# Experts' rows added in memory, one block at a time, to one zeroed row per token

## The reference, cut to what matters

```python
aff = sigmoid(einsum('bsd,de->bse', x, wa))
topk_p, topk_i = top_k(aff, 2)                  # two of 16 experts for each token
topk_p = topk_p / sum(topk_p, axis=-1, keepdims=True)
combine = sum(one_hot(topk_i, 16) * topk_p[..., None], axis=2)
routed = einsum('bsed,bse->bsd', experts_all(x, rg, rgb, rw1, rb1, rw2, rb2), combine)
shared = sum(experts_all(x, sg, sgb, sw1, sb1, sw2, sb2), axis=2)
return x + shared + routed
```

## Time and profile before

| What | Value |
|---|---|
| Median of 3 runs | 1137.9 us (1137.3 to 1138.25) |
| Profiled execution, its own time | 1144.85 us |
| Its span, first to last instruction | 1143.1 us |
| Mean granted clock of PE | 0.944 |
| PE busy | 1029.8 us (90%) |
| DVE, ACT, POOL busy | 845.9 us, 684.2 us, 582.2 us |

### The profile page before, as it was taken

The page is one execution under the profiler, slowest core; times in us unless marked ns, Lnnn a source line. Parts: engine busy times, 40 slices in busy tenths (PEclk is TensorE's granted clock), DMA queues, the critical chain, the costliest instruction groups (busy, mean ns, idle before and its releaser), DMA issues. The chain is left out here.

```text
span 1143.1 us, 24593 instructions
## 1 busy us (share of the span) xinstructions
PE 1029.8 (90%) x9092; PEld 771.7 (68%) x9175; DVE 845.9 (74%) x1480; ACT 684.2 (60%) x1203; POOL 582.2 (51%) x635
## 2 busy tenths in 40 slices
PE   4899998689998998878999988789996999999997
PEld 4677776634443776557877766687673888888874
DVE  5589999869998788757888866698746455556548
ACT  4565773779886656567888764574543345545431
POOL 5444445425544344458778885303873355555520
PEclk9999999789999999979999998659999899999999
DMA  8584431869886223232222210764986577678879
GB/s 318 176 256 122 160 116 38 158 174 237 221 226 177 87 72 104 68 89 56 65 71 63 57 30 1 257 226 181 203 249 224 165 239 242 236 246 281 303 264 352
DMA packets 133705, 194.60 MB, mean 170 GB/s; under 512 B 67990, under 2 KB 70204, under 8 KB 132792
## 3 DMA queue, kind: packets, MB, share of 16 engines
q1 hardware_dynamic: 117256, 149.45, 43.3%
q0 software_dynamic: 8544, 24.68, 7.0%
q10 hardware_dynamic: 7792, 18.96, 5.3%
HBM read 127.47 MB, written 44.48 MB: 150 GB/s over the span
## 5 line engine op out<-in xcount | busy, mean ns | idle before, releaser
L470 PE MATMUL ps_y<-kv,toep 128*128 128x288 f32 x640 | 156.5, 407 | 5.2 <-DMA toep<-taps_padded 3.2
L470 PEld LDWEIGHTS ps_y<-kv,toep 128*128 128x128 f32 x640 | 121.2, 190 | 40.0 <-DMA toep<-taps_padded 4.7
L164 POOL TENSOR_TENSOR kv<-kx 128x1024 f32<-128x1024 f32 x32 | 60.6, 1893 | 85.9 <-DVE outT L524 37.7
L1808 DVE TENSOR_REDUCE at_negmax<-ps_s 128x4 f32<-128x1024 f32 x64 | 78.1, 1220 | 32.0 <-PE ps_s L1859 32.0
L2684 POOL DMA_INDIRECT expert_results<-e_yo,target x47 | 69.7, 1482 | 58.1 <-ACT e_yo L2735 58.1
L1141 PEld LDWEIGHTS ps_eg<-e_xT,e_w 128*128 128x128 bf16 x1128 | 69.0, 100 | 15.1 <-DVE e_w L2789 2.5
L1141 PE MATMUL ps_eg<-e_xT,e_w 128*128 128x128 bf16 x1128 | 73.1, 223 | 4.0 <-DVE e_xT L2796 4.0
L1141 PE MATMUL ps_eu<-e_xT,e_w 128*128 128x128 bf16 x1128 | 72.2, 221 | 0.0
L2789 DVE COPY e_w<-expert_weights 128x4096 bf16 x47 | 57.7, 1227 | 19.3 <-issue 19.3
L2802 DVE SCALAR_TENSOR_TENSOR e_y<-ps_eu,e_bias,e_y 128x128 f32<-128x128 f32 x94 | 28.7, 346 | 55.1 <-PE ps_eu L1141 52.7
L2679 POOL DMA_INDIRECT e_rows<-token_rows,token x45 | 43.5, 967 | 49.9 <-PE ps_ex L2886 43.7
(11 more groups left out here) (450 smaller groups left out, 3086.8 us busy)
## 6 DMA issues: line engine op xcount, KB each, us to landing
e_parts<-down_parts SPq DMA_DIRECT2D x47, 512.0 KB
w_raw<-in_L_ffn_w ACTq DMA_DIRECT2D x32, 512.0 KB, 4.3
toep<-taps_padded SPq DMA_DIRECT2D x32, 256.0 KB, 3.5
f_draw<-in_L_ffn_rw SPq DMA_DIRECT2D x16, 512.0 KB, 4.5
down_parts<-f_dparts SPq DMA_DIRECT2D x16, 512.0 KB, 2.9
expert_weights<-expert_results SPq DMA_DIRECT2D x16, 512.0 KB, 11.2
x_res<-in_x SPq DMA_DIRECT2D x4, 1024.0 KB
c_in<-in_ctx SPq DMA_DIRECT2D x4, 1024.0 KB, 14.3
```

Of the source, the lines that this page charges most:

```text
L164: pool.tensor_tensor(pairs[:, :, :, 0:HD0], x[:, :, 0:HD0].unsqueeze(2).broadcast_to([P, ROWS_N, WIDE, HD0]), sliding_rows(x, 0, 1, WIDE), ...
L470: last = pe.matmul(y[:, l * B:(l + 1) * B, :, WIDE - 1:], toep[h % 2][:, (DC - 1 - l + m) * P:(DC - l + m) * P], kv[h % 2][:, m * B:(m + 1 ...
L1808: dve.tensor_reduce(negmax[u % 2][:, :].rearrange("p (j q) -> p j q", j=2), psS[:, :, :, :], AX.X, ALU.max, negate=True).then_inc(max_read, 1)
```

## The change

`expert_results` now has one row per token. A scatter adds its 128 rows in memory to what stands there (`compute_op=ALU.add`) instead of writing them. As both experts of a token address the same row, `target` is taken from the token's number after the wrap by 2048, and POOL waits before scatter(j) until scatter(j - 1) has landed. The 2048 rows are set to zero beforehand by 16 transfers of 256 KB from a zeroed tile, four in each of four steps of attention (u = 3, b = 1 to 4), on SP. At the end SP loads 8 transfers instead of 16 and DVE makes one addition per chunk instead of two.

```diff
@@ attention
-        bo = sb("at_bo", [P, D], F32)
+        bo, nothing = sb("at_bo", [P, D], F32), sb("at_nothing", [P, D], F32)
...
+        zero_rows = k.scratch["results"][0:TOK, :].rearrange("(t p) d -> t p d", p=P)
...
+            sp.wait_ge(nothing_set, 1)
             for b, u in STEPS:
                 q = b + 1
+                if u == 3 and 1 <= b <= 4:
+                    for t in range((b - 1) * NT // 4, b * NT // 4):
+                        sp.dma_start(zero_rows[t, :, :], nothing[:, :]).then_inc(results_zeroed, 16)
...
+            sp.wait_ge(results_zeroed, 16 * NT)
...
             pool.memset(bo[:, :], 0.0).then_inc(bias_zeroed, 1)
+            pool.memset(nothing[:, :], 0.0).then_inc(nothing_set, 1)
@@ routing
-                link(dve.tensor_copy(target[:, :], targetf[:, :]), wait=False)
                 link(dve.tensor_scalar(wrap[:, :], targetf[:, :], float(TOK), float(TOK), ALU.is_ge, ALU.mult))
                 link(dve.tensor_tensor(targetf[:, :], targetf[:, :], wrap[:, :], ALU.subtract))
+                link(dve.tensor_copy(target[:, :], targetf[:, :]), wait=False)
@@ experts
-        got = late(2 * NT * D).rearrange("p (t s d) -> p t s d", t=NT, s=2)
+        got = late(NT * D).rearrange("p (t d) -> p t d", t=NT)
...
             def scatter(j):
                 pool.wait_ge(out_ready, j + 1)
+                if j:
+                    pool.wait_ge(stored[(j - 1) % 2], 16 * ((j - 1) // 2 + 1))
                 pool.indirect_dma_start(out=k.scratch["results"], out_offset=bass.IndirectOffsetOnAxis(ap=target[:, j:j + 1], axis=0),
-                                        in_=yo[j % 2], in_offset=None).then_inc(stored[j % 2], 16)
+                                        in_=yo[j % 2], in_offset=None, compute_op=ALU.add).then_inc(stored[j % 2], 16)
...
             for c in ORDER:
-                for slot in range(2):
-                    sp.dma_start(got[:, c * ST:(c + 1) * ST, slot, :], results[c, slot, :, :, :]).then_inc(got_loaded[c], 16)
+                sp.dma_start(got[:, c * ST:(c + 1) * ST, :], results[c, :, :, :]).then_inc(got_loaded[c], 16)
...
-                dve.wait_ge(got_loaded[ORDER[n]], 32)
-                dve.tensor_tensor(x[:, tiles, :], x[:, tiles, :], got[:, tiles, 0, :], ALU.add).then_inc(first_added, 1)
-                dve.wait_ge(first_added, n + 1)
-                dve.tensor_tensor(x[:, tiles, :], x[:, tiles, :], got[:, tiles, 1, :], ALU.add).then_inc(done, 1)
+                dve.wait_ge(got_loaded[ORDER[n]], 16)
+                dve.tensor_tensor(x[:, tiles, :], x[:, tiles, :], got[:, tiles, :], ALU.add).then_inc(done, 1)
```

More of the change, by code:

```diff
@@ L1618, in stage_attention @@
         maxes_high, ones_copied, bias_zeroed, bias_high, bias_low, shift_ready = (sem(n) for n in ("mxh", "oc", "bz", "bh", "bw", "xs"))
-        stacked, k_loaded = sem("st"), sem("kl")
+        stacked, k_loaded, nothing_set, results_zeroed = (sem(n) for n in ("st", "kl", "ns", "rz"))
+        zero_rows = k.scratch["results"][0:TOK, :].rearrange("(t p) d -> t p d", p=P)
         block = ctx.enter_context(nc.Block())
@@ L2651, in stage_experts @@
             sem(n) for n in ("lgu", "lge", "lyf", "lyh", "lyl", "ldp", "lsa", "ldo", "lst", "lxt", "lx"))
-        got_loaded, first_added = [sem(f"lg{i}") for i in range(CH)], sem("lfa")
+        got_loaded = [sem(f"lg{i}") for i in range(CH)]
         space = W[:, :, :, :, :].rearrange("p e h c f -> p (e h c f)").bitcast(F32)
@@ L2665, in stage_experts @@
         late_x = [late_xT[:, :, :, :], late(ST * DC * P, BF16).rearrange("p (s h d) -> p s h d", s=ST, h=2)]
-        results = k.scratch["results"][0:2 * TOK, :].rearrange("(s i t p) d -> i s p t d", s=2, p=P, t=ST)
+        results = k.scratch["results"][0:TOK, :].rearrange("(i t p) d -> i p t d", p=P, t=ST)
         mid_dram = k.scratch["mid"].rearrange("(t p) d -> t p d", p=P)
@@ L3063, in program @@
                "slots": nc.dram_tensor("slot_table", [NBLK * BLK, 2], F32, kind="Internal").ap(),
-               "results": nc.dram_tensor("expert_results", [2 * TOK + NBLK * BLK, D], F32, kind="Internal").ap()}
+               "results": nc.dram_tensor("expert_results", [TOK + NBLK * BLK, D], F32, kind="Internal").ap()}
     build(nc, ins, out, scratch)
```

## The result

The changed kernel takes 1209.01 us (1206.05 to 1217.74, 4 runs) against 1137.76 us: a ratio of 1.0639, with a 95% interval of 1.0584 to 1.0694. It is 71 us slower. The direction was forecast, the size was not: 31 us were. The time lies just under the upper end of the stated range, 1212 us.

The account below looks back on a forecast made before the run. PE was taken to bound the block loop at 4.42 us a block, DVE the end. The terms 18.6 + 17.8 - 4 - 3.7 + 1.7 + 0.5 = +30.9 gave 1168.8 us, range 1141 to 1212.

Parts of the forecast that it names:

- only at the loads of x: Block loop: the wait between scatters binds only in blocks loading x; +5 to +8 us, 1143 to 1146 us; chance 0.21.
- the full second round trip: Block loop: adding costs a second transfer, landing after 6.5 us; +92, 1230 us; chance 0.14 with everything above 1195.
- The cheap adding: Block loop: by the skill's pages an adding scatter lands after about 3.2 us, the wait hidden in every block; 1134.8 us.
- the third rival: Block loop: the wait never binds, only DVE's end and the memset count; -3.2 us, 1134.7 us; chance 0.11.
- the term of "1.2 us": Each scatter: adding costs 0.85 us for reading old rows plus 0.35 for read before write and POOL's restart.
- the pace L = 5.0 us: Blocks 0 to 31: issue to landing takes 3.8 + 1.2 = 5.0 us against 4.42 a block; +18.6 us.
- The stretch with x loads: The 12 blocks loading x: 5.9 us each against 4.42, +17.8 us; the last three blocks 0.
- The 4 us that the loop absorbs: Block loop, once: a gather lands about 4 us before PE's transposes need it; -4 us.
- the 3.7 us of DVE's end: Program end: three DVE additions of 1.23 us fewer behind the last low part; -3.7 us.
- the +1.7 us of late loads: Program end: result loads start late, so DVE's low part of the second late expert reaches PE late; +1.7 us.
- Zeroing at nothing: Attention: the 16 zeroing transfers of 256 KB are hidden; 0 us, or 13.6 us of the engines if not.
- the memset: Attention's start: one more POOL memset of 128x512, 0.52 us, ahead of its first product; +0.5 us.

Follow-up runs that it names:

- the three buffers: Changed kernel with three buffers for the scaled rows instead of two, ACT waiting for the scatter three blocks back: 1209.7 us, ratio 1.0653 to the kernel before.
- both ways tried: Kernel before, each token's two rows added together for the last three chunks, by POOL (1138.2 us, ratio 1.0005) or by adding DMA transfers (1138.3 us, 1.0029).

## Why the prediction was wrong in size

**Right.** The mechanism: the chain of landings binds all through the loop, with the wait for the scatter before as its link, and PE idles for `e_rows`. One sign failed to the letter: POOL's idle time was to bear the name of the scatter before and not ACT's, and the profile put 35 of 47 waits down to ACT, which the three buffers explain. The rivals in which the chain binds nowhere or only at the loads of x are excluded, and so is the full second round trip (6.5 us a block). The cheap adding (L about 3.2 us) is excluded too: no adding scatter landed in less than 4.4 us. (The 1134.8 us given with it and the 1134.7 of the third rival are one sum.) The landing itself was forecast well: 3.8 us plain, where 3.6 were measured with the wait and no adding; 5.0 us with adding, where 5.0 is the median.

**The step that failed is the restart of POOL in the term of "1.2 us", and with it the pace L = 5.0 us.** The read that must end before its write and the restart of POOL were put at 0.35 us together, and the sum for blocks 0 to 31 was 32 x 0.58 = 18.6 us. Measured is 5.91 - 4.42 = 1.49 us over 31 steps, +46 us. Landing alone took the whole 5.0 us; the restart of 0.77 us came on top of it at every step, and the mean landing of 5.14 us gives the other 0.14 of the 0.91 us that the pace was short. So the restart explains most of what was missing.

How the landing came by its 1.4 us over the plain one (5.0 for 3.6) is not shown in parts. The pass over the old rows was put at 0.85 us of the engines and is 1.0 to 1.2; the issue takes 1.55 us instead of 0.96 where nothing disturbs POOL, which no row of before could show. These two together are more than 1.4, so they overlap in part, and that the forecast's 0.85 + 0.35 comes near the 1.4 is partly luck.

**The stretch with x loads** was put at 5.9 us a block. Its 12 steps, from scatter 31 to scatter 43, are 6.42 us each in the trace of after (1081.04 to 1158.09) and 4.52 in that of before (1038.95 to 1093.21): 22.8 us lost, where 17.8 were forecast. Landing is 5.3 us in the median there, 5.65 in the mean, below the 5.9 forecast; again it is the restart that lifts the step. The last three steps, put at nothing, went from 3.49 to 5.67 us each, +6.5.

**The once-only terms.** The 4 us that the loop absorbs, the 3.7 us of DVE's end and the +1.7 us of late loads made -6.0 together, and the last scatter to the end measures -6.6. This agreement is luck. PE begins its late experts at 1162.53 us, 12.6 us ahead of the last scatter, where it was 1.5 us before (1102.16): the scatters fell back by 11.0 us against PE. Of these, 6.5 are the last three steps, which therefore cost PE nothing, and 4.5 are what the loop absorbed, for 4 forecast. But from there to its last matmul PE takes 40.4 us instead of 32.7, +7.7 where +1.7 was forecast: the wait of 5.56 us, and 1.9 us for 12 matmuls at the lower clock, for which the sum had no term. DVE's end gave 3.8, for 3.7 forecast, and is 0.6 us behind PE, for 0.7. Zeroing at nothing was right, and the memset, put at +0.5 us, was hidden too.

Together: 45.9 + 22.8 - 4.5 + 7.7 - 3.8 and 0.5 from DVE's last of these additions to the end make 68.6 us, which is +75.2 for first to last scatter and -6.6 behind it, against 71 in the medians.

**Why one and not the other.** The wait alone costs 0.6% (about 1% without the shorter end that this kernel has), the adding alone 0.6%, both 6.4%. PE's 4.42 us per block hide any step of the chain up to that length. A plain landing and POOL's restart stay just under it outside the x loads; adding scatters that need not wait overlap one another. Only an adding scatter that must land before the next one goes exceeds it, and then the excess is paid at each of 46 steps.

No version that keeps both experts' rows was found faster than the kernel before. What the shorter end is worth (0.37%) is known; both ways tried to have it without the chain gave it back.

## What to carry to other kernels

Before a pipeline of independent transfers is made a chain, set the full step (issue, landing, and the issuing engine's restart) against the time per block: below it the chain was free here, above it the excess is paid at each block. Add the restart to the landing and don't fold it into another term: it was measured at 0.77 us. Price an adding transfer in DMA time as two plain ones or a little more (here 1.9 to 2.1 us against 0.85 for 256 KB scattered, 2.8 against 1.4 for 512 KB direct), and let at least two be in flight, with separate targets. Of POOL's waits ahead of one issue, try the one that is satisfied last in the first place; here that gave about 1%. A wait of PE near the end can cost more than its length, since the clock may be at its lower level behind it (5.30 us for 2.76). And when the chain names an engine with a free buffer's worth of slack, give it that buffer before believing it.

## What the runs showed of the hardware that was not expected

- The order of two waits on POOL, one long satisfied and one for a landing, changes the gap from the landing to the next issue by 0.50 us: 0.77 us when that wait stands second, 0.27 us when it stands first. Most of it was lost again, as landings took 0.4 us longer, for a reason that is not known.
- An adding scatter of 128 rows of 2 KB is issued as 64 more packets, takes 0.6 us longer to issue and 1.0 to 1.2 us more of the 16 DMA engines than a plain one, and lands after 5.0 us instead of 3.6 when each waits for the one before. In mid-loop, without the wait, it lifts the DMA share from 0.70 to 0.93 with no more GB/s in the profile, so that the share and not GB/s shows what it costs.
- Additions on POOL and DVE at the same time, both with operands in SBUF, cost DVE 3.2 us for 1.23.
- After PE had waited 3.67 us its granted clock was 0.50 for the next 12 matmuls (5.30 us for 2.76), and 0.58 after a wait of 5.56 us (4.70 us).
